# The low part of conv1's crossed rows goes by GpSimd instead of by the DMA queue, from the fourth image on

## What is computed

```
xn   = (x - mean) / sqrt(var + 1e-5)                   # per image and channel
gate = softmax(xn.mean((-2, -1)) @ gate_w.T + gate_b)  # 7 experts
kw1  = einsum('be,eoihw->boihw', gate, experts_w1) + conv1_w ; kw2, kb1, kb2 likewise
out1 = relu(conv3x3(xn, kw1) + kb1)
out  = x + xn + conv3x3(out1, kw2) + kb2
```

## Time and profile before

| | |
|---|---|
| Median of 3 runs | 345.15 us (344.61 to 346.08) |
| The profiled execution | 345.82 us, of which the span in the trace is 344.0 us |
| Mean granted TensorE clock | 0.982 |
| Busy: PE, DVE, ACT, POOL | 308.9, 268.4, 255.9, 185.9 us |
| Moved by DMA | 60.90 MB, mean 177 GB/s |
| The chain that ended last | PE 66%, DVE 8%, DMA 8%, ACT 5%, issue 5%, SP's queue 4%, POOL 3% |

### The profile page before, as it was taken

The page is one execution under the profiler, slowest core; times in us unless marked ns, Lnnn a source line. Parts: engine busy times, 40 slices in busy tenths (PEclk is TensorE's granted clock), DMA queues, the critical chain, the costliest instruction groups (busy, mean ns, idle before and its releaser), DMA issues.

```text
span 344.0 us, 8153 instructions
## 1 busy us (share of the span) xinstructions
PE 308.9 (90%) x3225; PEld 218.6 (64%) x3225; DVE 268.4 (78%) x586; ACT 255.9 (74%) x304; POOL 185.9 (54%) x202
## 2 busy tenths in 40 slices
PE   1289999774699999999999999999999999999993
PEld 1276866441477787777677768677767767555552
DVE  5587869799498989888898989797988889582432
ACT  2368799659489797969797988879796979775710
POOL 5146704588366584838484858567483848630000
PEclk9999999997699999999999999999999999999998
DMA  9987828929995998999998979999899993845055
GB/s 178 166 184 166 182 56 176 238 42 214 246 214 134 212 195 192 218 221 182 204 220 203 219 181 213 213 209 187 191 209 221 183 203 91 197 105 139 1 142 134
DMA packets 110372, 60.90 MB, mean 177 GB/s; under 512 B 103166, under 2 KB 105470, under 8 KB 110334
## 3 DMA queue, kind: packets, MB, share of 16 engines
q1 hardware_dynamic: 109536, 59.79, 83.1%
q10 hardware_dynamic: 798, 0.60, 0.8%
HBM read 19.47 MB, written 18.87 MB: 111 GB/s over the span
## 4 chain that ended last, share of the span: by engine, by line
PE 66%; DVE 8%; DMA 8%; ACT 5%; issue 5%; SPq 4%; POOL 3%; ACTq 0%; DVEq 0%
PE pg L410 64%; DMA wts<-wts 7%; DVE stats L738 2%; SPq L249 2%; POOL a L1071 2%; DMA img<-in_x 2%; DVE wts L831 1%; PE pset L377 1%; ACT a L590 1%; DVE wts L846 1%; SPq L299 1%; DVE img L867 1%; SPq L256 1%; ACT wts L628 1%; ACT c L654 1%
## 5 line engine op out<-in xcount | busy, mean ns | idle before, releaser
L410 PE MATMUL pg<-a,wts 128*64 128x480 f16 (+1 forms) x1440 | 290.0, 361 | 9.5 <-DMA wts<-wts 7.9
L410 PE MATMUL pg<-c,wts 128*64 128x480 f16 (+1 forms) x1440 | 291.3, 365 | 4.3 <-ACT a L644 4.3
L410 PEld LDWEIGHTS pg<-c,wts 128*64 128x64 f16 x1440 | 152.5, 109 | 52.1 <-ACT a L644 4.0
L410 PEld LDWEIGHTS pg<-a,wts 128*64 128x64 f16 x1440 | 153.0, 109 | 44.9 <-DMA wts<-wts 10.0
L1071 POOL TENSOR_TENSOR a<-xh,a 128x576 f16<-128x576 f32 x64 | 78.6, 1261 | 39.4 <-ACT xh L575 21.6
L654 ACT COPY c<-a 64x2352 f32<-64x2352 f32 (+2 forms) x48 | 71.8, 1497 | 2.3 <-DVE a L852 1.9
L867 DVE SCALAR_TENSOR_TENSOR img<-pg,img 128x480 f32<-128x480 f32 (+1 forms) x80 | 48.4, 634 | 23.8 <-PE pg L410 22.8
L791 DVE SCALAR_TENSOR_TENSOR mix<-bank,gate,mix 128x386 f32<-128x386 f32 x84 | 63.1, 752 | 2.0
L1094 POOL TENSOR_SCALAR img<-img,col 128x1152 f32<-128x1152 f32 x32 | 55.4, 1739 | 1.5
L644 ACT ACTIVATE a<-pg,col 128x480 f16<-128x480 f32 x80 | 52.8, 660 | 0.0
L1059 POOL TENSOR_TENSOR col<-col,minus_half 128x1 f32<-128x1 f32 x16 | 13.2, 825 | 72.0 <-DVE col L764 72.0
(11 more groups left out here) (67 smaller groups left out, 148.1 us busy)
## 6 DMA issues: line engine op xcount, KB each, us to landing
img<-in_x SPq DMA_DIRECT2D x56, 288.0 KB, 6.7
c<-a SPq DMA_DIRECT2D x26, 588.0 KB, 6.6
out<-img SPq DMA_DIRECT2D x60, 180.0 KB, 3.0
out<-img SPq DMA_DIRECT2D x60, 108.0 KB, 2.7
c<-a SPq DMA_DIRECT2D x24, 147.0 KB, 2.5
wts<-wts SPq DMA_DIRECT2D x28, 96.0 KB, 3.1
img<-in_x SPq DMA_DIRECT2D x16, 144.0 KB, 5.1
out<-img SPq DMA_DIRECT2D x4, 120.0 KB, 2.1
```

Of the source, the lines that this page charges most:

```text
L410: last = nc.tensor.matmul(pg[g][side * 64:side * 64 + 64, at:at + nb * W].rearrange("p (b w) -> p b w", w=W), wts[s.number % WSETS][kind][ ...
```

## The change

From the fourth image on the low part of `c1` is no longer made by SP's transfer. A new step `cross_low(t)` on POOL, right behind `low_part(t)`, copies it in two instructions, one for each half of the partitions, each of 64 partitions by 1176 fp32 words (the 2352 fp16 numbers of a partition read as words). POOL waits for its own low part first, and after each copy for the end of that copy. SP's `cross1(t)` moves the high part alone, in two transfers of half the size, and waits for `hi1_ok` in place of `lo1_ok`. PE waits, before conv1's group 0, for a new semaphore `low_crossed` too. The first three images are as before.

```diff
+        low_crossed = sem("low_crossed")
...
             def cross1(t):
-                sp.wait_ge(lo1_ok, t.number + 1)
+                sp.wait_ge(hi1_ok, t.number + 1)
                 for half, d0 in ((0, 0), (1, 1)):
-                    sp.dma_start(halves(c1[t.parity])[half][:, :, d0:d0 + NB, :].rearrange("p a b w -> p a (b w)"),
-                                 halves(a1[t.parity])[half].rearrange("p a b w -> p a (b w)")
+                    sp.dma_start(halves(c1[t.parity])[half][:, HI, d0:d0 + NB, :].rearrange("p b w -> p (b w)"),
+                                 halves(a1[t.parity])[half][:, HI].rearrange("p b w -> p (b w)")
                                  ).then_inc(crossed1[t.ring], 16)
...
             def conv1_group(s, g):
                 if g == 0:
                     pe.wait_ge(w_crossed[s.ring], 32 * crossings(s))
                     wait_low_part(s)
+                    pe.wait_ge(low_crossed, 2 * (s.number - EARLY + 1))
...
+            def cross_low(t):
+                pool.wait_ge(lo1_ok, t.number + 1)
+                r = RP // 2
+                for half in range(2):
+                    d, a = (halves(k[t.parity])[half][:, LO].rearrange("p b w -> p (b w)").bitcast(F32) for k in (c1, a1))
+                    nc.gpsimd.tensor_copy(d[:, half * r:(half + NB) * r], a[:, :]).then_inc(low_crossed, 1)
+                    pool.wait_ge(low_crossed, 2 * (t.number - EARLY) + half + 1)
...
             def slot(s):
                 run(residual_bias, s, 0, 2)
                 run(low_part, s, 1, 3)
+                run(cross_low, s, 1, 3)
                 run(coefficients, s, 2, 4)
                 run(residual, s, 0, 2)
```

## The result

The changed kernel takes 340.16 us (339.98 to 340.31, 4 runs), the kernel before in the same comparison 345.04: a ratio of 0.985, 95% interval 0.9823 to 0.9877. That is 1.5% faster, where 1.0% was forecast (341.7 us). The direction was right and the time lies inside the range, 0.3 us above its lower end, but the gain of 4.9 us is nearly half as large again as the sum of 3.5. As the experiments show, one step of the sum failed, and the gain of another does not need the reason given for it.

The account below looks back on a forecast made before the run. PE was taken as the bound, held up by crossed weights late on SP's full queue. Gains of 2.5 us in the repeated part and 1.0 at the fourth image took 345.15 to 341.7 us; range 339.9 to 344.8.

Parts of the forecast that it names:

- the sum of 3.5: Whole kernel: 2.5 us gained in the repeated part plus 1.0 us at the fourth image.
- What bounds the kernel: PE, 90% busy, waits for crossed weights 7.9 us in all; SP's queue is full; undisturbed slots take about 18.2 us.
- The copies: Two copies a slot on POOL, 1.5 us each, hidden in its wait for DVE with 1.7 us to spare.
- The contention: Repeated part: the second copy lies on DVE's line 852 and makes the chain to `veps_ok` 0.7 us later.
- The block of 1.4 us: Repeated part: by the skill's rule, line 852 would wait for the rest of the second copy, 1.4 us.
- 588 KB a slot leave the queue: Repeated part: less traffic lands weights in 2.7 us or less instead of 4.7, so PE's waits go, 2.5 us.
- The fourth image: Start of conv1: earlier, half-sized crossing outweighs coefficients 2.3 us late; PE restarts at 87.7 instead of 88.75, 1.0 us gained.
- the slow stretch of the clock would move with the restart and cost the same: Fourth image: the 3.9 us of half-speed matmuls behind PE's restart stay behind it, with no gain or loss.
- rival E: Fourth image: a shorter standstill keeps PE's clock up or restores it earlier, up to 2 us more gain, 339.7 us; chance 0.03.
- the late coefficients: Fourth image: copies delay the fifth image's coefficients 2.3 us, to 77.8, and through ACT and DVE `w_ok` to 84.9.

Follow-up runs that it names:

- second pair of executions: Both kernels run once more unchanged, one execution each, to see where the slow clock falls: kernel before 345.53 us, changed kernel 340.78 us.
- Experiment 6: Kernel before with every crossing from the fourth image on split by parts into four transfers of 294 KB, released late, all bytes, no copies: 342.46 us.
- Experiment 9: Kernel before with the crossing in four transfers of 294 KB split by rows, each with both parts of half the rows, released late: 345.64 us.
- experiment 1: Kernel before with the crossing split by parts; at the fourth image the high part goes at `hi1_ok`, ahead of the load; all bytes, no copies: 339.57 us.
- experiment 2: Changed kernel without POOL's two copies and PE's wait for them, so part of the computation is left out: 337.92 us.
- experiment 3: Kernel before, queue unchanged, with POOL's two copies added into a tile nobody reads, with the same waits: 346.68 us.
- experiment 7: Changed kernel with SP's crossing of the high part waiting for `lo1_ok` again; half the bytes and the copies stay: 340.82 us.
- experiment 4: Kernel before with 17 unused matmuls on PE between the second image's conv2 and the fourth image's conv1: 344.38 us.
- experiment 5: Kernel before with the earlier, split crossing for the fourth image alone; later images as before, same bytes, no copies: 342.80 us.
- experiment 12: Changed kernel run once more, unchanged, one execution, for the place of the slow clock: 340.78 us.
- experiment 8: Changed kernel with POOL's order swapped: coefficients of the next image first, then the copies: 337.35 us.

## Why the prediction was half right

**What bounds the kernel** held for the repeated part: without PE's waits for the crossed weights a slot fell to 18.22 us, where 18.2 was named. At the fourth image the clock was to be had too.

**The copies** held in size: 1.16 to 1.57 us, mean 1.34, for 1.5 taken. In the repeated part they hid in POOL's wait for DVE, with 2.11 us to spare (1.7 said). The contention was 0.6 us for 0.7 taken, but on another operation. Line 855 took 0.69: it began at 164.42, before the second copy at 164.66, and it is this copy that took 1.48 us, where the first took 1.16. Line 758, which reads two small SBUF tiles, took 0.79, with a median of 0.17 in the kernel before: it began at 165.37, while the copy ran, and ended at 166.16, where the copy ended at 166.14. The Trainium skill's rule on two SBUF inputs ("SBUF — State Buffer", section "Who interferes with whom") agrees with line 758, which was held for all that was left of the copy. The block of 1.4 us that the prediction worked out for line 852 did not come, as that operation began before the copy and not after it.

**The repeated part**, step "588 KB a slot leave the queue": the size was nearly right (2.8 us for 2.5; in the second pair of executions 1.8), but the bytes need not have left for it. The change also turned a transfer of two stretches a partition into one of one stretch and half the size, which I did not see as an edit. Experiment 6 does only that, with all the bytes, and its ten slots are 2.67 us shorter than those of the kernel before, or 1.67 shorter than in its second execution. Experiment 9, as many transfers of the same size with two stretches, has nothing. No run halves the bytes and keeps two stretches, so that the bytes alone would have failed is not shown. Halving the bytes as well as splitting brings the landing from 3.8 down to 2.2 us, which PE does not need in most slots. What they are worth is seen without copies (experiments 1 and 2: 1.7 us), most of it at the fifth image, where PE is early and waits 1.4 us in the one and not in the other.

**The fourth image**, step "the slow stretch of the clock would move with the restart and cost the same": this is the step that failed. The slow stretch did not move with the restart: it came ahead of it, and the run from restart to mark got 0.85 us shorter, where the prediction had 0. It was rival E at a chance of 0.03, in another form: the clock was full behind the restart because the slow stretch lay elsewhere. The range holds the measured time by 0.3 us only, and it was drawn for the price of the copies and not for this step, so that it holds is in part luck. I had followed the late coefficients over ACT to `w_ok`, rightly (77.22 for 77.8 and 84.0 for 84.9, restart 86.80 for 87.7), and had not asked who else waits for them: PE does, at `logits` of the fifth image, 3.5 us, ahead of the last two groups of conv2. So PE's long standstill is cut in two, and the slow clock falls on groups whose delay PE's wait for the weights takes up, and is over when the fourth image begins. In all four traces of kernels with the copies ahead of the coefficients (the changed kernel twice, experiments 3 and 7) a slow stretch begins at 78.4 to 80.0 and none lies behind the restart. That it is the wait for `gwp` which brings it there is argued and not shown: experiment 2 has a slow stretch at 80.9 without that long wait. From restart to mark the kernels with the slow stretch behind the restart take 19.7 to 21.1 us (the kernel before twice, experiments 4, 5, 6 and 9), those without it 18.4 to 18.6 (experiments 1, 2 and 3). The changed kernel's 19.45 is neither (nor are the 19.46 and 19.44 of experiments 12 and 7): its clock is full, but 0.82 us of it is the wait for line 758 at 93.31.

The sum then reads, in spans: 1.46 us of earlier restart (1.0 said), 0.85 of clock less new waits (0 said), 2.80 in the repeated part (2.5 said), and 0.49 of ordinary difference between two executions. In medians it is 4.9.

**What stays open.** Why the transfers of two stretches a partition hold up those behind them: landing and waits show that they do, the trace not why, and the number of stretches, their length and the size of a transfer are not fully told apart. And what decides whether the slow clock comes before or behind a restart; only where it came is shown. The length of the last standstill alone does not decide it: experiment 5 stood still for 2.35 us, the changed kernel for 2.19, and only experiment 5 was slow behind it.

## What to carry to other kernels

When work is put in front of a step, list every engine that waits for that step, not only the one on the known chain; here the same two copies cost 2 us ahead of the coefficients and nothing behind them (340.16 and 337.35 us, and 337.92 without copies). When a diff halves a transfer, look at what else it does to the transfer: here splitting it by parts, with all the bytes kept, gave as good as all that the repeated part gained. And before work is moved to another engine to relieve a queue, try the queue with simpler transfers: 342.46 us came from splitting alone, 339.57 from splitting and an earlier issue, with nothing on GpSimd.

## What the runs showed of the hardware

Four transfers of 294 KB with one stretch of 4704 bytes a partition let the small transfers behind them land within 3.8 us, four with two stretches of 2352 bytes in 4.5, two of 588 KB with two stretches of 4704 in 4.7 (experiments 6 and 9, and the earlier trace rows, all at the weights near 250 us). A DVE operation with two SBUF inputs that began while a GpSimd copy ran ended 0.02 us after the copy, and a copy that began while such a DVE operation ran took 1.48 us instead of 1.16 (the changed kernel, 163 to 166 us). Around the fourth image the clock was slow for 3.4 us (experiment 4, from 90.4) up to 10.2 us (the kernel before, from 82.4). In experiments 1 and 8 that stretch lay ahead of everything told here (from 70.3 and 69.8). Between the two executions of the kernel before, the stretch around the restart began 5.0 us apart (82.4 and 87.4), and the second had another one from 70.3 to 73.7.
